# Layer 1's pooling: where the token rows are split into high and low parts, and when batch 0's last denominators are computed

## The reference

```python
attn_in = jnp.tanh(jnp.einsum('bsd,da->bsa', hidden, W1) + b1)
scores = jnp.einsum('bsa,a->bs', attn_in, v)
mask = jnp.where(pt == 0, prefix_m[None], jnp.where(pt == 1, postfix_m[None], cloze_m[None]))
masked_scores = jnp.where(mask, scores[:, None, :], NEG_INF)
p = jax.nn.softmax(masked_scores, axis=-1)
cnt = jnp.sum(mask, axis=-1).astype(hidden.dtype)
pooled = jnp.einsum('bjl,bld->bjd', p, hidden) / cnt[..., None]
# the router behind it: logits = x @ Wr + br; idx = argmax(logits); gate = softmax(logits)[idx]
```

## Time and profile before

| | |
|---|---|
| median of 3 runs | 1234.48 us (1232.47 to 1237.12) |
| the profiled execution, its own time | 1233.81 us |
| its span, first to last instruction | 1232.0 us |
| busy PE, PEld, DVE | 1073.0, 1002.6, 928.6 us |
| busy ACT, POOL | 641.9, 515.3 us |
| mean granted TensorE clock | 0.92 of full |
| chain that ended last | PE 73%, DVE 13%, issue 5%, DMA 4%, ACT 3% |

### The profile page before, as it was taken

One profiled execution on the slowest core, in us unless ns is written; L12 is line 12 of the kernel. 1 busy time (PEld: TensorE's weight loads), 2 busy tenths in 40 slices (PEclk: granted clock), 3 DMA queues, 4 the chain that ended last, 5 costly groups with the idle time before them and its releaser, 6 DMA issues.

```text
span 1232.0 us, 25727 instructions
## 1 busy us (share of the span) xinstructions
PE 1073.0 (87%) x7824; PEld 1002.6 (81%) x7824; DVE 928.6 (75%) x1603; ACT 641.9 (52%) x1360; POOL 515.3 (42%) x347
## 2 busy tenths in 40 slices
PE   5689866999999999999996657999768968889896
PEld 4478766999999999999995547999658866778785
DVE  6766796888888888888873866877548766767695
ACT  3435325667676676766753345766247635223221
POOL 5000004787888887888851104552126740000000
PEclk8789887999999999999997668999879988999998
DMA  7300127677778677777733136673356754030202
GB/s 192 110 18 4 59 98 236 202 229 231 236 220 258 214 239 243 209 254 232 227 77 86 34 111 241 236 261 90 103 186 211 245 159 161 20 100 23 91 14 69
DMA packets 82621, 191.90 MB, mean 156 GB/s; under 512 B 16883, under 2 KB 57603, under 8 KB 70275
## 3 DMA queue, kind: packets, MB, share of 16 engines
q1 hardware_dynamic: 60642, 151.01, 36.4%
q0 software_dynamic: 21920, 40.21, 13.3%
HBM read 158.01 MB, written 33.18 MB: 155 GB/s over the span
## 4 chain that ended last, share of the span: by engine, by line
PE 73%; DVE 13%; issue 5%; DMA 4%; ACT 3%; DVEq 0%; POOL 0%; another core or an unknown queue 0%; SPq 0%; POOLq 0%; ACTq 0%
PE ps L823 23%; PE ps L824 22%; PE ps L825 22%; PE ps L952 2%; DVE hidden_lo L1777 2%; PE ps L835 1%; DMA w_raw<-z_rows,slot_rows 1%; DVE featA_lo L1777 1%; DVE featB_lo L1777 1%; DVE w_lo L1777 1%; DMA z_tok<-y_rows 1%; DVE x_tok L2118 1%; DVE z_tok L2514 1%; DMA z_rows<-z_tok 0%
## 5 line engine op out<-in xcount | busy, mean ns | idle before, releaser
L1518 ACT ACTIVATE hidden_f<-ps,b_block 128x256 f32<-128x256 f32 x432 | 222.0, 514 | 175.7 <-PE ps L825 167.9
L707 POOL DMA_INDIRECT x_tok<-z_gate_rows,slot_rows x76 | 209.0, 2750 | 232.2 <-DVE slot_rows L1952 159.6
L1519 ACT ACTIVATE hidden_hi<-ps,b_block 128x256 fp32r<-128x256 f32 x432 | 224.2, 519 | 0.0
L1777 DVE TENSOR_TENSOR hidden_lo<-hidden_f,hidden_hi 128x512 fp32r<-128x512 f32 x284 | 183.9, 691 | 31.7 <-ACT hidden_hi L1519 17.7
L823 PE MATMUL ps<-w_hi,featA_hi 128*128 128x256 f32 (+1 forms) x628 | 181.1, 288 | 9.5 <-DVE featA_lo L1777 4.1
L824 PE MATMUL ps<-w_lo,featA_hi 128*128 128x256 f32 (+1 forms) x628 | 180.1, 287 | 0.0
L825 PE MATMUL ps<-w_hi,featA_lo 128*128 128x256 f32 (+1 forms) x628 | 180.0, 287 | 0.0
L823 PE MATMUL ps<-featB_hi,hidden_hi 128*128 128x256 f32 x616 | 175.8, 285 | 3.5 <-DVE hidden_lo L1777 3.5
L824 PE MATMUL ps<-featB_lo,hidden_hi 128*128 128x256 f32 x616 | 173.7, 282 | 0.0
L825 PE MATMUL ps<-featB_hi,hidden_lo 128*128 128x256 f32 x616 | 172.5, 280 | 0.0
L735 POOL DMA_INDIRECT x_rows<-w_raw,slot_rows x76 | 128.5, 1690 | 36.1 <-issue 21.9
(11 more groups left out here) (480 smaller groups left out, 2947.2 us busy)
## 6 DMA issues: line engine op xcount, KB each, us to landing
scratch<-in_L_w SPq DMA_DIRECT2D x48, 1024.0 KB
z_tok<-in_L_w SPq DMA_DIRECT2D x29, 1024.0 KB
x_tok<-in_L_w SPq DMA_DIRECT2D x19, 1024.0 KB
b_block<-in_L_ffn_b POOLq DMA_DIRECT2D x60, 128.0 KB
z_tok<-y_rows SPq DMA_DIRECT2D x12, 512.0 KB, 5.5
z_tok<-in_L_w SPq DMA_DIRECT2D x12, 512.0 KB
scratch<-in_L_w SPq DMA_DIRECT2D x12, 512.0 KB
z_rows<-z_tok SPq DMA_DIRECT2D x8, 512.0 KB, 2.9
```

The lines of the kernel that those rows point to most:

```text
L707: gp.indirect_dma_start(XBL[L][:, k, tt, :], None, ZD if L else ZD0, bass.IndirectOffsetOnAxis(ap=TOK[:, q * BTT + tt:q * BTT + tt + 1], a ...
L1518: act.activation(HF[:, f // 2, part], ps, func, bias=b1)
L1519: act.activation(HTh[:, k, f // 2, part], ps, func, bias=b1).then_inc(s_hhi[L], 1)
L1777: return nc.vector.tensor_tensor(out, full, hi.bitcast(F32), ALU.subtract)
```

## The change

Chunks 2 and 3 of the token rows are split by DVE too, directly behind chunks 0 and 1, with the same instructions. ACT's two casts, GpSimd's two subtractions and the semaphore between them are gone. TensorE waits once, ahead of batch 0, for the ones, all four chunks and the router's columns. `normalize(0, 1)` is moved from the end of batch 0's pass to a place behind `carry_in(1)`, ahead of `row_maxima(1)`; `normalize(1, 1)` keeps its place.

```diff
@@ block.gpsimd, behind layer 0's blocks
-            for c in (2, 3):
-                gp.wait_ge(s_act, c - 1)
-                gp.tensor_tensor(xr_chunk(XRl, c), X[:, c * TPC:(c + 1) * TPC, :], xr_chunk(XRh, c).bitcast(F32),
-                                 ALU.subtract).then_inc(s_xb2, 1)
@@ block.tensor, pooling
             pe.wait_ge(s_sc_sb, B)
+
+            pe.wait_ge(s_xr, 1 + NC + 1)
             for b in range(B):
-
-                if b:
-                    pe.wait_ge(s_xb2, NT + 2)
-                else:
-                    pe.wait_ge(s_xr, 4)
@@ block.scalar, behind the score rows
-            for c in (2, 3):
-                act.activation(xr_chunk(XRh, c), X[:, c * TPC:(c + 1) * TPC, :], ACT.Copy).then_inc(s_act, 1)
@@ block.vector
-            for c in (0, 1):
+            for c in range(NC):
                 link(nc.vector.tensor_copy(xr_chunk(XRh, c), X[:, c * TPC:(c + 1) * TPC, :]))
                 lo(xr_chunk(XRl, c), X[:, c * TPC:(c + 1) * TPC, :], xr_chunk(XRh, c)).then_inc(s_xr, 1)
@@
             for b in range(B):
                 carry_in(b)
+                if b:
+                    normalize(0, 1)
                 row_maxima(b)
@@
                 normalize(b, 0)
-                normalize(b, 1)
+            normalize(1, 1)
             dve.wait_ge(s_den, 2 * B)
             top1(1)
```

More of the change, by code:

```diff
@@ L264, in build @@
         s_dve = sem("dve_step")
-        s_act = sem("act_step")
         TR = ["x0", "z0", "x1", "x2", "x3", "rare"]
```

## The result

| | before | after |
|---|---|---|
| median of 11 runs | 1232.94 us (1231.92 to 1237.12) | 1228.88 us (1224.62 to 1232.20) |
| ratio, 95% interval | | 0.9964 (0.9950 to 0.9979) |
| profiled execution: its time, its span | 1233.81, 1232.0 us | 1229.72, 1227.9 us |

The medians differ by 4.1 us; the forecast was 4.7 us. Two further measurements of the same kernel, beside the experiments, gave 0.9971 (0.9951 to 0.9991) and 0.9978 (0.9960 to 0.9996). As shares of 1234 us the three ratios are 4.4, 3.6 and 2.7 us; the medians of the two further ones differ by 3.2 and 2.3 us. What happened ahead of the stage drops out of these.

What follows compares the result with a forecast made beforehand. TensorE bounds the whole span; DVE's list and one wait for TensorE set the stage. Lock 3.0 + wait 1.7 + reading 0.1, less clock 0.1, gives 4.7 us: profiled 1229.1 us, forecast 1229.8 us, range 1226.0 to 1235.0 us.

Steps and rivals of the forecast that it cites:

- Part 1: Ahead of layer 1's first scores: DVE's two extra splits, 3.82 us, fit its 4.82 us wait; path cost 0.
- Part 2: Batch 0's arguments: without GpSimd's subtractions, which block DVE over shared SBUF ports, batch 1's scans start 3.0 us earlier.
- Part 3: Batch 0's second normalize behind batch 1's carries: DVE's 1.71 us wait for TensorE goes; row maxima 4.8 us earlier in total.
- ACT's exponentials: Batch 1, queued behind the moved normalize's copies: done about 703.1 us, DVE asks at 703.7 us, 0.6 us of cover.
- batch 1's clock: TensorE in batch 1: a clock rise 1.2 us later costs 0.1 to 0.4 us; 0.1 us taken.
- (a): Before batch 0's second normalize: DVE still waits for TensorE, 3 to 4 us gain remains, 1231.2 us; chance 0.12.
- (b): Ahead of the first scan: the splits stretch beyond the 4.82 us wait by 1 to 2 us, 1231.5 us; chance 0.05.
- (c): Layer 1's blocks and batch 1: fewer matmuls at the lower clock, 1.4 to 2.4 us, 1227.8 us; chance 0.15.
- (d): Layer 1's pooling: the clock doesn't rise in either batch, 4 to 5 us slower than before, 1239 us; chance 0.06.

Runs made afterwards that it cites:

- uncovered: The changed kernel with DVE splitting chunks 2 and 3 behind batch 0's scans instead of ahead of them; ratio to before 1.0007.
- the dead subtractions: The changed kernel with ACT's two casts and GpSimd's two subtractions put back into buffers nothing on the path waits for; ratio to before 1.0008.
- move-only run: The kernel before with only batch 0's second normalize moved behind batch 1's carries, ACT and GpSimd still splitting chunks 2 and 3; ratio 0.9992.
- second and third profile: The unaltered changed kernel measured twice more, as yardstick for other runs; ratios to before 0.9971 and 0.9978.
- fillers ahead of the blocks: The changed kernel plus 20 unused TensorE matmuls of 128x128 behind the slot tokens, before layer 1's blocks; ratio to before 0.9967.
- late memsets: The changed kernel plus two unread GpSimd memsets, held until the router's columns are written; one execution, last normalize 40.06 us behind the first scan.

## Why the prediction was right

**Part 1, the splits in the wait: right.** 1.13 us of wait was left, forecast 1.0 us; uncovered, the same work costs 3.7 us, forecast 3.8 us.

**Part 2, the lock: right, in size and mechanism.** Batch 1's scans came 19.30 - 16.33 = 2.97 us earlier, forecast 3.0 us, and the dead subtractions brought 3.3 us back. The prediction took the place of the collision, the arguments, for fixed. The move-only run has it on the tensor_scalar and the one-column instruction behind it, for 3.3 instead of 3.0 us.

**Part 3, the move: right in the total, wrong in who gets the credit.** The row maxima came 4.87 us earlier, forecast 4.8 us. But the 1.7 us booked for the move is mostly the splits': with them TensorE's second half ends early enough that 0.73 us of wait is left without a move. The splits alone give 3.96 us, the move alone 1.60 us, both 4.9 us: the two share one wait. Part 2 of the prediction had the numbers for this (sums at 699.5 us, first normalize over at 698.9 us, so 0.6 us of wait), and didn't draw the conclusion. ACT's exponentials were no wait, as said.

**The term of the sum that was mis-sized: batch 1's clock.** Taken were 0.1 us, with 0.1 to 0.4 us as its cost if the rise came later. From the row maxima to the last normalize batch 1 took 15.11 us in before, and 15.47 and 15.51 us in the second and third profile of after, 0.4 us more; but 16.94 us in the first, 1.8 us more; two experiments with the same pooling (fillers ahead of the blocks, late memsets) took 16.8 us too. The cause there is one that the prediction did not name: the clock rose earlier than in before and fell within the second half. In the three profiles the stage, up to the blocks, gained 2.6 to 4.3 us, and the three measured ratios stand for 2.7, 3.6 and 4.4 us.

The late rise is in the second and third profile (5.7 us behind the start in the second), and it costs the 0.4 us foreseen; it is the early rise, with the fall inside the batch, that turned out dear.

**The rivals.** (a), a wait before the second normalize, did not occur in after. (b) fell: the splits fit. (c), a better clock handed on, did not show in the medians. (d), the clock low through the pooling, fell: it rose in both batches in every profile of after, though (d)'s place, batch 1, is where the missing microsecond went. That the two first profiles lie 4.1 us apart like the medians is in part chance: of these 4.1 us only 2.6 us arose between the first scan and the blocks, 0.4 us ahead of it and 1.1 us behind, where the kernels do the same. There is luck in the absolute forecast too: 1229.8 us stood on the median of 3 runs, 1234.48 us, and the median of 11 was 1232.94 us. From there the same sum gives 1228.2 us, against 1228.88 us measured.

## What to carry to other kernels

Work that GpSimd does "for free" beside a full DVE is not free where DVE is on the path: compare the same instruction with GpSimd busy and idle in one trace, and if one batch's row is five times the other's, the difference over the list estimates what moving the work into a wait of DVE can gain, as long as no other wait takes its place. When two parts of a change shorten the same wait, price them one after the other and not by adding. For a change of a few microseconds in a program of a millisecond, measure the distance between two landmarks around it; whole spans of single profiles moved by more than the change.

## What the runs showed of the hardware that was not expected

- Two GpSimd memsets back to back, which read nothing, held up a DVE tensor_scalar of 128x1022 by 3.1 us (3.88 instead of 0.74 us); later in the list they left four two-input instructions of 128x128 at 1.14 us.
- TensorE's clock can fall in the middle of a batch. In after it rose at 706.3 us and fell at 713.1 us, behind a pause of 1.0 us; in the kernel with the pause between the batches filled it was high from the start and fell at 714.5 us, behind pauses of 0.7 and 1.3 us. Where it rose late (second and third profile) TensorE had no such pause, and it fell only after the last carry. Batch 0 of before has the same picture (high from 693.2 to 700.0 us, TensorE pausing for 0.66 and 0.83 us at 694.5 and 697.1 us), and batch 1 of before the opposite one: no pause up to the last carry at 720.8 us, and high from 713.7 to 723.9 us. Whether the pauses are the cause is not settled: with them filled the clock held, in two profiles.
- A rise that comes early, with a fall before the batch is over, can so cost more than one that comes late: 16.9 against 15.5 us for the same batch.
